# Another order of the work of a pass on four engines, in the six attention and feed-forward layers of an eight-stage kernel

## The reference

```python
def attn_layer(x, Wqkv, qs, ksc, Wo):
    q, k, v = jnp.split(x @ Wqkv, 3, -1)          # 16 heads of 64
    q = l2norm(q) * qs
    k = l2norm(k) * ksc
    q = q * cos * scale + rotate_half(q) * sin * scale
    k = k * cos * inv + rotate_half(k) * sin * inv
    out = local_attention(q, k, v)                # window 32, looks one window back
    return out @ Wo

def ffn_layer(x, g, bln, W1, b1, W2, b2):
    xn = (x - mu) / jnp.sqrt(var + 1e-05) * g + bln
    a, gate = jnp.split(xn @ W1 + b1, 2, -1)
    return a * jax.nn.gelu(gate, approximate=False) @ W2 + b2

for i in range(6):
    x = attn_layer(shift_tokens(x), ...) + x
    x = ffn_layer(shift_tokens(x), ...) + x
```

## Time and profile before

| what | value |
|---|---|
| median of 3 runs | 4588.0 us (4586.9 to 4590.96) |
| the profiled execution | 4585.71 us, its span 4583.9 us |
| PE busy | 4024.2 us, 88% of the span |
| DVE busy | 3549.3 us, 77% |
| ACT busy | 2985.7 us, 65% |
| POOL busy | 2213.8 us, 48% |
| TensorE clock granted, mean | 0.933; in the layers 1.00 |

### The profile page before, as it was taken

The page is one execution under the profiler, slowest core; times in us unless marked ns, Lnnn a source line. Parts: engine busy times, 40 slices in busy tenths (PEclk is TensorE's granted clock), DMA queues, the critical chain, the costliest instruction groups (busy, mean ns, idle before and its releaser), DMA issues. The chain is left out here.

```text
span 4583.9 us, 117843 instructions
## 1 busy us (share of the span) xinstructions
PE 4024.2 (88%) x43247; PEld 2378.6 (52%) x43247; DVE 3549.3 (77%) x8496; ACT 2985.7 (65%) x5496; POOL 2213.8 (48%) x1392
## 2 busy tenths in 40 slices
PE   8969999999999999999999999999999954747645
PEld 5644555555555555555555555555555532535533
DVE  6878888888888888888888888888888846356441
ACT  3427777777777777777777777777777745635302
POOL 0006665666666666666566666656656500140006
PEclk9989999999999999999999999999999965868557
DMA  1012322322223322232222322233222200000202
GB/s 42 1 55 64 67 59 62 83 66 64 61 61 84 69 61 62 60 85 68 60 61 63 83 67 63 59 77 72 63 62 66 55 17 12 1 1 6 83 7 38
DMA packets 188120, 251.24 MB, mean 55 GB/s; under 512 B 88676, under 2 KB 129382, under 8 KB 187366
## 3 DMA queue, kind: packets, MB, share of 16 engines
q1 hardware_dynamic: 182054, 240.47, 22.5%
q0 software_dynamic: 5632, 4.33, 0.7%
HBM read 41.65 MB, written 14.30 MB: 12 GB/s over the span
## 5 line engine op out<-in xcount | busy, mean ns | idle before, releaser
L1246 POOL TENSOR_TENSOR f_rot_a<-f_rot_a,f_norm 128x1024 f32<-128x1024 f32 x384 | 730.8, 1903 | 947.2 <-DVE f_norm L1085 914.7
L1238 POOL TENSOR_TENSOR f_rot_a<-f_rot_a,f_rot_b 128x1024 f32<-128x1024 f32 x384 | 909.5, 2368 | 229.7 <-issue 197.2
L843 PE MATMUL f_bank<-f_w_vo,f_xs_t 128*32 128x512 f32 x6144 | 813.7, 601 | 42.6 <-ACT f_vo L1315 42.6
L1315 ACT ACTIVATE f_vo<-f_bank 128x512 f32<-128x512 f32 x768 | 457.0, 595 | 357.7 <-PE f_bank L843 347.4
L1306 ACT ACTIVATE f_squares<-f_bank 128x512 f32<-128x512 f32 x768 | 456.4, 594 | 271.6 <-PE f_bank L829 191.5
L1064 DVE TENSOR_TENSOR f_rot_a<-f_bank,f_rot 128x512 f32<-128x512 f32 x768 | 523.7, 682 | 80.4 <-DVE f_stat L1113 42.2
L1067 DVE TENSOR_TENSOR f_rot_b<-f_bank,f_rot 128x512 f32<-128x512 f32 x768 | 516.0, 672 | 0.0
L875 PEld LDWEIGHTS f_bank<-f_k_t,f_q_t 128*32 128x32 f32 x12288 | 329.1, 110 | 284.7 <-ACT f_k_t L1327 151.5
L1071 DVE TENSOR_REDUCE f_sums<-f_squares 128x16 f32<-128x1024 f32 x384 | 464.0, 1208 | 1.6
L1327 ACT ACTIVATE f_k_t<-f_bank 64x512 f32<-64x512 f32 x768 | 449.3, 585 | 4.8 <-PE f_bank L865 0.3
L1252 POOL TENSOR_TENSOR f_prob<-f_score,f_stat 128x512 f32<-128x512 f32 x384 | 400.1, 1042 | 96.4 <-DVE f_stat L1117 96.4
(11 more groups left out here) (446 smaller groups left out, 7227.1 us busy)
## 6 DMA issues: line engine op xcount, KB each, us to landing
f_vo_off<-f_vo SPq DMA_DIRECT2D x1152, 128.0 KB, 2.3
f_vo_off<-f_vo SPq DMA_DIRECT2D x384, 64.0 KB, 2.0
f_w_qk<-in_Wqk SPq DMA_DIRECT2D x12, 512.0 KB, 5.2
f_vo_dram<-f_vo_pair SPq DMA_DIRECT2D x48, 128.0 KB, 1.8
f_x_shifted<-s_all SPq DMA_DIRECT2D x48, 128.0 KB
f_x_shifted<-s_all SPq DMA_DIRECT2D x48, 127.0 KB
f_w_vo<-f_vo_dram SPq DMA_DIRECT2D x10, 512.0 KB, 4.0
e_w<-in_e_W SPq DMA_DIRECT2D x2, 2048.0 KB, 11.6
```

Source lines behind the costliest of these rows:

```text
L843: done = nc.tensor.matmul(bank[V][32 * w:32 * w + 32, :], x[:, at:at + 32], w_vo[:, 4 * g:4 * g + 4, w // 2, :], start=True, stop=True)
L1238: nc.gpsimd.tensor_tensor(rot_a[:, slot, :, :], rot_a[:, slot, :, :], rot_b[:, g, :, :], ALU.add).then_inc(rot_summed, 1)
L1246: nc.gpsimd.tensor_tensor(heads, heads, over(norm[:, 16 * g:16 * g + 16], [128, 16, HEAD_DIM]), ALU.mult).then_inc(qk_normed, 1)
L1315: nc.scalar.activation(vo[:, g, 2 * (t % 2) + j, :], flat(V), ACT.Copy).then_inc((va_copied, vb_copied)[j], 1)
```

## The change

Only the four `body` functions differ. The loop over rounds is gone; the 83 steps of a pass on PE, 79 on DVE, 26 on POOL and 80 on ACT are written out one by one, the same steps with the same waits, in another order. SP's order is the same. The whole of POOL's, and the places on PE and DVE that the next sections speak of:

```diff
@@ gpsimd, body(p): all of it
-                for r in range(PASS_TILES):
-                    if on(r - 1):
-                        scale(p, r - 1, 1)
-                    if on(r - 2):
-                        weigh(p, r - 2, 1)
-                    if r == 0 and has(p, 0):
-                        take_x(1, p)
-                    if r == 2 and has(p, -1):
-                        take_x(0, p + 1)
-                    if on(r):
-                        add_up(p, r, 0)
-                        scale(p, r, 0)
-                    if on(r - 1):
-                        weigh(p, r - 1, 0)
-                    if on(r):
-                        add_up(p, r, 1)
+                if live(p, -1):
+                    scale(p, -1, 1)
+                if live(p, -2):
+                    weigh(p, -2, 1)
+                if live(p, 0):
+                    add_up(p, 0, 0)
...
+                    scale(p, 0, 0)
+                if live(p, -1):
+                    weigh(p, -1, 0)
+                if live(p, 0):
+                    add_up(p, 0, 1)
+                    scale(p, 0, 1)
...
+                if live(p, 2):
+                    add_up(p, 2, 0)
+                if has(p, -1):
+                    take_x(0, p + 1)
+                if live(p, 2):
+                    add_up(p, 2, 1)
+                    scale(p, 2, 0)
+                    scale(p, 2, 1)
+                if live(p, 1):
+                    weigh(p, 1, 0)
...
@@ vector, body(p), from the end of tile 0's scores, and tile 2
+                    invert(0)
+                    highest(p, -1, 1)
+                if has(p, 2):
+                    normalise(p - 2)
...
+                if live(p, 1):
+                    rotate(p, 1, 1, 1, 0)
+                if has(p, 3):
+                    store(p - 3)
...
+                if live(p, 2):
+                    length(p, 2, 1)
+                    rotate(p, 2, 1, 0, 0)
+                    rotate(p, 2, 1, 0, 1)
+                    rotate(p, 2, 1, 1, 1)
+                    inverse_lengths(p, 2)
...
@@ tensor, body(p), tiles 2 and 3
+                if live(p, 1):
+                    turn_k(p, 1, 1)
+                if live(p, 2):
+                    project_q(p, 2, 1)
+                if has(p, 2):
+                    gate_proj(p - 2, 2)
+                if live(p, 0):
+                    mix(p, 0, 0)
+                if live(p, 2):
+                    values_a(p, 2, 0)
+                if live(p, 1):
+                    scores(p, 1, 1)
+                if live(p, 0):
+                    mix(p, 0, 1)
+                if live(p, 3):
+                    project_k(p, 3, 0)
+                if live(p, 2):
+                    values_b(p, 2, 0)
...
+                    turn_x(0, p + 1)
+                if live(p, 3):
+                    project_q(p, 3, 0)
+                if live(p, 2):
+                    values_a(p, 2, 1)
+                    turn_q(p, 2, 0)
+                if has(p, 2):
+                    up_proj(p - 2, 0)
```

More of the change, by code:

```diff
@@ new lines, in body @@
+                if has(p, 0):
+                    fold(p)
+                if live(p, 0):
+                    project_k(p, 0, 1)
+                if live(p, -1):
+                    scores(p, -1, 0)
+                    turn_q(p, -1, 1)
+                if live(p, 0):
+                    project_q(p, 0, 1)
+                    values_a(p, 0, 0)
+                if live(p, -2):
+                    mix(p, -2, 0)
+                    turn_prob(p, -2, 1)
+                if has(p, 0):
+                    pe.wait_ge(fold_made, p + 1)
+                    turn_x(1, p)
@@ new lines, in body @@
+                if live(p, -1):
+                    turn_k(p, -1, 1)
+                if live(p, 1):
+                    project_k(p, 1, 0)
+                if live(p, 0):
+                    values_b(p, 0, 0)
+                if live(p, -2):
+                    mix(p, -2, 1)
+                if live(p, 0):
+                    values_a(p, 0, 1)
+                if live(p, -1):
+                    scores(p, -1, 1)
+                if live(p, 0):
+                    turn_q(p, 0, 0)
+                if live(p, 1):
+                    project_q(p, 1, 0)
@@ new lines, in body @@
+                if live(p, 0):
+                    values_b(p, 0, 1)
+                if live(p, -1):
+                    turn_prob(p, -1, 0)
+                if live(p, 0):
+                    turn_k(p, 0, 0)
+                if live(p, 1):
+                    project_k(p, 1, 1)
+                if has(p, 3):
+                    down_proj(p - 3)
+                if live(p, 1):
+                    project_q(p, 1, 1)
+                if live(p, 0):
+                    turn_q(p, 0, 1)
+                    scores(p, 0, 0)
@@ new lines, in body @@
+                if has(p, 2):
+                    turn_normed(p - 2)
+                if live(p, 0):
+                    turn_k(p, 0, 1)
+                if live(p, 1):
+                    values_a(p, 1, 0)
+                if live(p, -1):
+                    turn_prob(p, -1, 1)
+                    mix(p, -1, 0)
+                if live(p, 0):
+                    scores(p, 0, 1)
+                if live(p, 1):
+                    values_b(p, 1, 0)
+                if live(p, 2):
+                    project_k(p, 2, 0)
@@ new lines, in body @@
+                if live(p, 2):
+                    turn_q(p, 2, 1)
+                    scores(p, 2, 0)
+                if live(p, 3):
+                    values_a(p, 3, 0)
+                if live(p, 1):
+                    mix(p, 1, 0)
+                    turn_prob(p, 1, 1)
+                if live(p, 2):
+                    turn_k(p, 2, 1)
+                if has(p, 2):
+                    up_proj(p - 2, 1)
+                if live(p, 3):
+                    values_b(p, 3, 0)
+                if live(p, 1):
+                    mix(p, 1, 1)
@@ L1022, in _ @@
+                if live(p, 2):
+                    scores(p, 2, 1)
             for p in range(LAST + 3):
```

515 lines of the change are left out of this document (346 added, 169 removed).

## The result

| | before | after |
|---|---|---|
| median | 4589.48 us (4586.9 to 4592.82, 4 runs) | 4553.74 us (4550.84 to 4554.98, 4 runs) |
| ratio to before | | 0.9921, 95% interval 0.9906 to 0.9936 |
| profiled span | 4583.9 us | 4549.0 us |
| TensorE clock granted, mean | 0.933 | 0.931 |

The kernel is 35.7 us faster, 0.8%. The forecast was 75 us, 4513. What happened is the case put second, with 4552 us: a second hold, at `normalise`. The range held the time; the forecast itself did not come true, and that the second case's number fits to 2 us is partly luck (its sum is looked at behind the experiments).

A forecast was written before the change was run, and what follows sets the result against it. PE was taken as the bound: pass 66.4 + 1.3 = 67.7, 1.6 less than 69.3; times 45 is 72, plus 3 at the start, 75; 4585.7 - 75 + 2.3 = 4513 us. Range for 8 in 10: 4452 to 4582.

The forecast's parts named there:

- the case put second: Rival: normalise on DVE held by add_up and scale, 5.0 us; pass 68.55, 4552 us; chance 0.26.
- The bound and the four waits: PE bounds; its waits at turn_normed (0.4), values and scores (together 1.7) and up_proj (0.5) go; pass 66.4.
- The hold at the inverse lengths: Tile 2: POOL's second add_up holds DVE's second small instruction, making DVE 2.2 late; PE waits 1.3 before turn_q (2,0).
- `normalise`: On DVE: two of four instructions start before add_up (0,1), one is held 2.4, the last passes before scale: 3.1 us.
- The rival's own price: With normalise at 5.0 us, PE waits 0.85 more between scores (-1,1) and project_q (1,1).
- The passes of the start: The two starting passes that have most of the steps gain 3 us.
- Slower through DVE at tile 3: Rival: DVE becomes the bound at tile 3; pass 69.7, 18 us slower, 4606 us; chance 0.12.
- its neighbour: The forecast case: hold at the inverse lengths, normalise at 3.1 us, pass 67.7, 4513 us; chance 0.44.

The follow-up runs named there:

- both edits: Changed kernel with POOL's scale (2,0) ahead of add_up (2,1), and add_up (0,1) waiting for normalise: 4455.68 us, in a later group 4463.86 us.
- The third experiment: Changed kernel with a memset of a scratch tile and its wait on POOL ahead of add_up (0,1): 4521.31 us.
- the sixth experiment: Kernel with both edits, and in passes 0 and 1 the orders of the kernel before on all four engines: 4461.0 us.
- the eighth kernel: Kernel with both edits plus three swaps on PE joining runs of 32-wide products, and weigh (-1,1) ahead of add_up (1,0) on POOL: 4449.8 us.
- the ninth: The eighth kernel plus a fourth join on PE, DVE rotations ahead of highest (-1,0), and ACT's copy_values ahead of a square: 4425.98 us.
- e1 to e4: Changed kernel with scale ahead of add_up, 4490.68 us; add_up waiting for normalise, 4516.88; both edits, 4455.68; only PE's and ACT's new orders, 5288.04.
- e5 to e10: POOL pause, 4521.31 us; both edits with old start, 4461.0; normalise moved, scale swapped, 4464.91; three joins, 4449.8; four joins, 4425.98; both edits again, 4463.86.

## Why the prediction was right and wrong

- **The bound and the four waits**: right. They are gone, and PE without waits needs 66.22 us in the run with both edits; the text had 66.4. A wait did cost more than its idle time, 0.37 us with 0.20 idle at `turn_normed` and 0.65 with 0.49 at `project_q` (1, 1). That the array empties and fills in the rest is how the text read it; the traces show the amounts.
- **The hold at the inverse lengths**: right in mechanism, place and size. 2.38 for the second of the nine, `inverse_lengths` 4.31 from the start of its first to the end of its last, PE's wait 1.3 as worked out. Removing it gave 1.26 a pass. What the text rested this on was only near: it took the 1.04 us of the later line in the earlier trace rows for one POOL operation, but the one beside it (L2179, from 0.07 us ahead of it) takes 1.26. The run showed the hold itself, 2.38 beside 2.37.
- **`normalise`**: wrong, and this is the step that failed: "Two of its four instructions start ahead of it by my placing." None did. My placing gave POOL 0.4 us between `weigh` and `add_up`, the 0.43 that stands ahead of an `add_up` in the earlier trace rows; the prediction doesn't show this step. But in that row it waits for a rotation of DVE. In the new order its inputs had long been there, and it followed `weigh` 1.00 us after that one's start. Counted from the `highest` that both sides have ahead of them (2055.51), `weigh` comes after 0.27 and `add_up` after 1.27, `normalise` after 1.33. So POOL was 0.06 ahead and not some 0.4 behind. The third experiment moved it by half a microsecond and got 3.15 us and 67.48 a pass, near the forecast's 3.1 and 67.7. The rival's own price, 0.85 on PE, was 0.65 to 0.73.
- **The passes of the start**: wrong in sign. 3 us of gain assumed in proportion, 10.6 lost. There PE has little or no feed-forward work, and in the changed kernel it waits 8.7 us for rotations of DVE (11 times) and 4.2 for `scale` (3 times), against 3.3 and 1.4 before. 6.4 us went with the holds and 5.1 with the order, by the sixth experiment; of the 6.4, some 1.6 may be the clock, the difference of the two profiles with both edits in the third pass. That the chains of DVE and POOL bound these passes is how I read it; no run shows it by itself.
- **Slower through DVE at tile 3**: did not happen; DVE's two waits in tile 1 are still 1.14 and 1.08 us.

The forecast's sum misses 0.56 in each of 45 passes, 25 us, and 13.6 at the start: 4513 + 39 = 4552.

That the second case also says 4552 is partly luck. Its mechanism was what happened, but its pass was 68.55 and not 68.26, 13 us too much in 45 passes, and its start gained 2 us where 10.6 were lost, 12.6 the other way. The two errors cancel.

The chances were the poorer part. A case that turns on 0.15 us of placing deserved as much as its neighbour, not 0.26 against 0.44.

## What to carry to other kernels

Where DVE and POOL both work in SBUF, look in the timeline for each short DVE instruction of a form that is seen held (here TENSOR_SCALAR from SBUF to SBUF, and in the earlier trace rows one with two SBUF inputs) at the start of a long POOL one: here it took as long as the whole POOL instruction (2.38 us beside 2.37, 2.41 beside 2.37) or no longer than alone (0.18, 0.34), by who started first, and swapping two POOL steps gave 1.26 us a pass, letting POOL wait for 1.28 us gave 0.73. A gap read from one row is a gap only where the same thing is waited for. And a gain per pass isn't a gain in the passes that fill the pipeline: three of them lost 10.6 us here while each later one gained 1.05, so they want their own sum.

## What the runs showed of the hardware

- A memset on POOL, which only writes, did not hold `normalise`. In the third experiment the memset (0.31 us) started 0.07 us ahead of the first instruction of `normalise`, and that one took 0.34 us as ever. No run tells why the memset leaves it free.
- The hold takes tiny operands: 128x32 int32, one input, 0.18 us alone, 2.38 beside `add_up`. In all 48 passes of the changed kernel it ends 0.04 us behind POOL's instruction, which takes 2.37, and DVE shows it as busy time.
- The two forms of DVE that take the most time here are not held. In the changed kernel `rotate`, with one input in a bank, and `length`, which reads SBUF alone, start again and again while POOL is in the middle of an instruction (in 44 passes 924 and 132 times), and no one of them takes longer for it (ns, shortest, median, longest):

```profile
L1160 DVE TENSOR_TENSOR f_rot_a<-f_bank,f_rot x768: 636/680/693, 344.9 to 3605.8; 128x512 f32<-128x512 f32 x192
...
L1167 DVE TENSOR_REDUCE f_sums<-f_squares x384: 1156/1208/1222, 347.5 to 3601.1; 128x16 f32<-128x1024 f32 x192
```

- Runs of 32-wide products that PE does directly one after another, instead of with a full-width block between, saved 0.2 to 0.3 us a time (0.29 and 0.23 for two joins of the eighth kernel, 0.82 for the four of the ninth).
- With both edits the kernel was profiled twice, 4457.5 and 4463.3 us; the steady passes are the same, and the last stage, from its first to its last PE instruction, took 71.2 and 79.2. The traces show two sorts of this stage, whatever the change in the layers: 71.2 to 71.4 us in the profiles of before, after and e1 to e4, 77.5 to 79.3 in those of e5 to e10. In the longer sort the granted clock is at half for 6.8 us some 20 us into the stage. In the second of the two profiles PE had just stood idle for over 1 us ahead of each of three transposes (at 4364.3, 4365.7 and 4367.1), and the half clock begins at 4367.2. PE's busy time in the stage is 3.2 us more there (67.9 and 64.7), the rest is idle time. What PE waits for at these transposes stays open. The medians of the kernel before are 5 to 7 us higher in the same two groups, so times of different groups compare to no better than some 8 us.
